# Chunked cross-attention on one core: masks added on VectorE with the score copy, row maximum subtracted on GpSimd

## The chip, the core and the metric

One core of a Trainium2 chip runs the whole program. The metric is the device time of one execution in microseconds. Five engines work side by side, each with its own in-order queue: TensorE (PE, matmuls and its weight loads PEld), VectorE (DVE), ScalarE (ACT), GpSimd (POOL) and SyncE (SP, which issues all DMAs here). Engines wait for each other through semaphores that count completed instructions.

## The reference

The inputs are x and ctx (32 batches, 256 channels, 2048 tokens), a mask (32, 1, 2048), and the weights and biases of the projections. Tokens attend within chunks of 64, with 8 heads of 32 channels.

```
q, k, v = ctx^T W_in^T + b_in                      # 256 channels each
s   = q k^T / sqrt(32) + (0 where mask > 0 else -1e9)   # per chunk of 64 tokens and head
out = softmax(s) v ;  out = (out W_out^T + b_out) * mask + x
out = (out - mean) * rsqrt(var + 1e-5)             # mean and var over the 2048 tokens of a channel
```

## The kernel before, in words

A batch is cut into 4 blocks of 512 tokens, and each block into 2 units of 256 tokens (4 chunks). There are 8 units `u` in a batch, 256 in the run, and 128 blocks. Every engine runs the same outer loop (`batches`, `steps`): one step for each unit `u`, with work for neighbouring units and blocks. With `j = u // 2`, a step with even `u` is called an even step here, and one with odd `u` an odd step. The projections are full-size matmuls in three terms (high times high, low times high, high times low parts); scores, transposes and probabilities times values are small float32 matmuls.

TensorE's queue in step u: the scores of unit u+1 (mask rows L327, then 64 matmuls L334 into the four banks of `score_bank`); in an even step the keys of block j+1 (`project_k`, L262, two halves f=0 and 1), in an odd one the output projection of block j-1 (`project_out`, L310, two halves); probabilities times values of unit u-1 (L368); the transposes of unit u (`turn`, L349, into the other half of each score bank); in an even step the values of block j+1 (`project_v`, L293, two halves), in an odd one the queries of block j+2 (`project_q`, L262). Half f of `project_v` waits for `k_f_done` of half f, because it writes the bank that `keys` empties. `project_out` f waits for the copies of the values out of that bank (`v_done[f]`). `project_q` f waits for `y_done` of half f and for `ctx_lo`. The scores of a unit wait until the transposed probabilities of the unit two before have been copied (`prob_t_done`).

ScalarE's queue, which the diff doesn't touch:

```python
if u >= BLOCKS: normalise(B, u - BLOCKS, 0)      # L462
if h == 0: keys(B, j + 1, 0)                     # L443
exponentials(B, u + 1)                           # L412
if h == 0: keys(B, j + 1, 1)                     # L443
high_attention(B, u - 1)                         # L429, o_hi
turned_probs(B, u)                               # L419, prob_t
split_ctx(B, j + 2, 1) if h == 0 else split_ctx(B, j + 3, 0)   # L404
if u >= BLOCKS: normalise(B, u - BLOCKS, 1)      # L462
values(B, j + 1) if h == 0 else both queries(B, j + 2, f)      # L452 or L436
```

VectorE's queue in step u: `less_maximum` of unit u+1 (reduce L572, then subtraction L576, both reading the scores from PSUM); in an even step `masked_keys` (L565) and `statistics` (two L623; after it, at u = 2, `mean_and_variance`), in an odd one `output` for both halves (L614); `low_attention` of unit u-1 (L594, waits for `o_hi`); `reciprocal_sums` of unit u+1 (L583, waits for the exponentials, then L587); in an even step the copy of half of the values (L603); at u = 3 `mean_shift` (L640, L642), which waits for GpSimd's `rstd`.

GpSimd's queue in step u: at u = 3 first `reciprocal_std` (L531); in an even step two `add_residual` (L525) and `low_ctx(j+2, 1)` (L515), in an odd one `low_ctx(j+3, 0)`; then `divide` of unit u+1 (L508). `low_ctx` waits for ScalarE's `split_ctx` of the same part.

Of the kernel before, what the change touches and what calls it, by code (L numbers as in the profile page):

```python
# [5 lines left out]
F32 = mybir.dt.float32  # L6
F32R = mybir.dt.float32r
BF16 = mybir.dt.bfloat16
# [30 lines left out]
def attention_kernel(nc, x, ctx_in, mask, w_in_t, b_in, w_out_t, b_out, out):  # L39
    stack = ExitStack()  # L40
    with stack:
# [22 lines left out]
        ones_row = sb("ones_row", [P, CHUNK], BF16)  # L64
# [8 lines left out]
        neg_rows = sb("neg_rows", [P, 2, BLOCK], BF16)  # L73
# [45 lines left out]
        rows_done = sem("rows_done")  # L119
        max_done = sem("max_done")  # L120
# [129 lines left out]
        def _(pe):  # L250
# [63 lines left out]
            def scores(B, u):  # L314
# [3 lines left out]
                if h == 0:  # L318
                    pe.wait_ge(neg_done, count(B, BLOCKS, j + 1))
                    pe.wait_ge(q_f_done, count(B, 2 * BLOCKS, 2 * (j + 1)))  # L320
                    pe.wait_ge(k_f_done, count(B, 2 * BLOCKS, 2 * (j + 1)))
                wait(pe, less_done, count(B, UNITS, u))
                wait(pe, prob_t_done, count(B, UNITS, u - 1))
                for r in range(ROWS):
                    masked = neg_rows[r * DH:r * DH + 1, j % 2, h * UNIT:(h + 1) * UNIT]
                    for f in range(HALVES):
                        pe.matmul(score_bank[f * CHUNK:(f + 1) * CHUNK, r, row_part], ones_row[r * DH:r * DH + 1, :],  # L327
                                  masked, start=True, stop=False, skip_group_check=True)
                for c in range(CPU):
                    tokens = slice(h * UNIT + c * CHUNK, h * UNIT + (c + 1) * CHUNK)  # L330
                    for r in range(ROWS):
                        head = slice(r * DH, (r + 1) * DH)
                        for f in range(HALVES):
                            last = pe.matmul(score_bank[f * CHUNK:(f + 1) * CHUNK, r, c * CHUNK:(c + 1) * CHUNK],  # L334
                                             q_f[head, j % 2, f, tokens], k_f[head, j % 2, f, tokens], start=False,
                                             stop=(c == CPU - 1), skip_group_check=True)
                last.then_inc(rows_done, 1)

            def turn(B, u):
# [4 lines left out]
                if unit_there(B, u + 1):  # L344
                    pe.wait_ge(less_done, count(B, UNITS, u + 2))
# [28 lines left out]
            pe.wait_ge(pool_const, 4)  # L374
# [119 lines left out]
        def _(pool):  # L494
# [5 lines left out]
            pool.memset(ones_row[:, :], 1.0).then_inc(pool_const, 1)  # L500
            pool.wait_ge(pool_const, 4)

            def divide(B, u):
# [4 lines left out]
                pool.tensor_tensor(part, part, slots(recip[:, u % 2, :]), ALU.mult).then_inc(norm_done, 1)  # L508

# [23 lines left out]
            def steps(B):  # L533
                for u in range(UNITS):
                    j, h = u // UPB, u % UPB
                    if u == 3:
                        reciprocal_std(B)
                    if h == 0:
                        add_residual(B, j - 2, 0)
                        add_residual(B, j - 2, 1)  # L540
# [3 lines left out]
                    divide(B, u + 1)  # L544
# [4 lines left out]
        def _(dve):  # L549
# [10 lines left out]
            def masked_keys(B, n):  # L560
# [3 lines left out]
                wait(dve, rows_done, count(B, UNITS, UPB * (n - 1)))  # L564
# [3 lines left out]
            def less_maximum(B, u):  # L568
                if not unit_there(B, u):
                    return  # L570
                dve.wait_ge(rows_done, count(B, UNITS, u + 1))
                dve.tensor_reduce(row_max[:, :].rearrange("p (r c) -> p r c", c=CPU), rows, AX_X,  # L572
                                  ALU.max).then_inc(max_done, 1)
                wait(dve, turned, count(B, UNITS, u - 1))
                dve.wait_ge(max_done, count(B, UNITS, u + 1))
                dve.tensor_tensor(prob[:, u % 2, :, :, :], rows, slots(row_max[:, :]),  # L576
                                  ALU.subtract).then_inc(less_done, 1)
# [109 lines left out]
```

## Time and profile before

| | |
|---|---|
| median of 3 runs | 2226.42 us (2226.14 to 2228.15) |
| profiled execution, its own time | 2225.78 us |
| its span, first to last instruction | 2224.0 us |
| PE busy | 2189.0 us (98%) |
| DVE busy | 1755.9 us (79%) |
| ACT busy | 1380.2 us (62%) |
| POOL busy | 1149.8 us (52%) |
| mean granted TensorE clock | 0.997 |

The table's busy times overlap, since the engines run side by side. In the timelines below each row gives the start in microseconds from the start of the span, the duration, the engine, the line of the kernel, the operation, the tensors (out<-in), the shapes, and a count where equal instructions that touch are merged. A bracket at the end is idle time of the engine just before the row, with what ended it.

### The profile page before, as it was taken

The page shows a single profiled execution, that of the slowest core. Times are in us where ns is not written, and L with a number is a line of the kernel's source. Part 1 is how long each engine was busy: PE and PEld are TensorE (multiplying, and loading weights), DVE is VectorE, ACT ScalarE, POOL GpSimd, SP SyncE. Part 2 cuts the span into 40 slices and gives each one's busy share as a digit, 9 for nine tenths or more (in the row PEclk, how much of TensorE's full clock was granted, in tenths as well). Part 3 has the DMA queues.
Part 4 walks back from the last instruction along what each step waited for, and adds up shares of the span by engine and source line. Part 5 has one row for each costly group of instructions (what it writes and reads, how often), then busy time and mean ns, then how long its engine had stood idle before and what let it go on. Part 6 is the DMA issues. An engine that isn't in the chain of part 4 may idle for free.

```text
span 2224.0 us, 97930 instructions
## 1 busy us (share of the span) xinstructions
PE 2189.0 (98%) x44552; PEld 1835.7 (83%) x44552; DVE 1755.9 (79%) x2213; ACT 1380.2 (62%) x1921; POOL 1149.8 (52%) x808
## 2 busy tenths in 40 slices
PE   7999999999999999999999999999999999999996
PEld 6888888888888888888888888888888888888885
DVE  4778877887878788778887788787788877887875
ACT  4566566666666666666666666666666566666664
POOL 3455555555555555455545554555455555555553
PEclk9999999999999999999999999999999999999998
DMA  3223333323333233333333332333333333323322
GB/s 133 79 93 113 114 111 111 120 98 104 109 121 121 93 108 120 112 115 115 102 103 111 120 121 88 111 114 118 116 102 108 110 111 112 121 97 108 107 92 96
DMA packets 126172, 242.23 MB, mean 109 GB/s; under 512 B 10561, under 2 KB 10817, under 8 KB 125761
## 3 DMA queue, kind: packets, MB, share of 16 engines
q1 hardware_dynamic: 125760, 235.97, 32.6%
q8 instruction: 352, 5.77, 1.1%
q14 instruction: 60, 0.48, 0.1%
HBM read 168.82 MB, written 67.11 MB: 106 GB/s over the span
## 4 chain that ended last, share of the span: by engine, by line
PE 97%; DVE 1%; ACT 1%; issue 0%; POOL 0%; DMA 0%; SPq 0%; POOLq 0%; ACTq 0%; DVEq 0%
PE proj_bank L262 33%; PE proj_bank L310 17%; PE proj_bank L293 16%; PE score_bank L349 12%; PE o_bank L368 9%; PE score_bank L334 8%; PE score_bank L327 3%; DMA ctx_raw<-ctx 0%; ACT y L462 0%; POOL prob L508 0%; POOL y L525 0%; DVE prob L576 0%; DVE row_max L572 0%; POOL ctx_lo L515 0%; DVE o_lo L594 0%
## 5 line engine op out<-in xcount | busy, mean ns | idle before, releaser
L515 POOL TENSOR_TENSOR ctx_lo<-ctx_raw,ctx_hi 128x512 fp32r<-128x512 f32 x256 | 330.3, 1291 | 1032.4 <-ACT ctx_hi L404 1032.4
L572 DVE TENSOR_REDUCE row_max<-score_bank 128x16 f32<-128x1024 f32 x256 | 313.3, 1224 | 305.0 <-PE score_bank L334 305.0
L412 ACT ACTIVATE prob<-prob 128x1024 f32<-128x1024 f32 x256 | 271.0, 1058 | 380.0 <-DVE prob L576 380.0
L508 POOL TENSOR_TENSOR prob<-prob,recip 128x1024 f32<-128x1024 f32 x256 | 487.0, 1902 | 23.1 <-DVE recip L587 20.9
L262 PE MATMUL proj_bank<-ctx_hi,w_hi 128*128 128x512 f32 x1024 | 342.4, 416 | 5.1 <-POOL ctx_lo L515 4.3
L576 DVE TENSOR_TENSOR prob<-score_bank,row_max 128x1024 f32<-128x1024 f32 x256 | 313.6, 1225 | 28.4 <-DVE row_max L572 2.4
L525 POOL TENSOR_TENSOR y<-y,x_raw 128x512 f32<-128x512 f32 x256 | 324.4, 1287 | 7.5 <-DVE y L614 7.4
L262 PE MATMUL proj_bank<-ctx_hi,w_lo 128*128 128x512 f32 x1024 | 317.8, 391 | 0.0
L262 PE MATMUL proj_bank<-ctx_lo,w_hi 128*128 128x512 f32 x1024 | 316.7, 391 | 0.0
L583 DVE TENSOR_REDUCE sums<-prob 128x16 f32<-128x1024 f32 x256 | 308.8, 1206 | 1.9 <-ACT prob L412 1.9
L419 ACT ACTIVATE prob_t<-score_bank 128x1024 f32<-128x1024 f32 x256 | 263.0, 1027 | 59.6 <-PE score_bank L349 53.6
L443 ACT ACTIVATE k_f<-proj_bank,b_cols 128x512 f32<-128x512 f32 x256 | 174.1, 680 | 193.0 <-PE proj_bank L262 193.0
L349 PE MATMUL score_bank<-ident,prob 128*128 128x128 f32 x2048 | 279.5, 279 | 3.9 <-DVE prob L576 3.9
L368 PEld LDWEIGHTS o_bank<-prob_t,v_f 64*32 64x32 f32 x16384 | 178.4, 105 | 91.0 <-issue 90.8
L349 PEld LDWEIGHTS score_bank<-ident,prob 128*128 128x128 f32 x2048 | 219.7, 141 | 27.6 <-issue 4.2
L334 PE MATMUL score_bank<-k_f,q_f 32*64 32x64 f32 x16384 | 230.7, 228 | 0.0
L594 DVE TENSOR_TENSOR o_lo<-o_bank,o_hi 128x512 fp32r<-128x512 f32 x256 | 174.5, 682 | 67.8 <-ACT o_hi L429 67.7
L262 PEld LDWEIGHTS proj_bank<-ctx_hi,w_lo 128*128 128x128 f32 x1024 | 192.9, 188 | 42.1
L262 PEld LDWEIGHTS proj_bank<-ctx_lo,w_hi 128*128 128x128 f32 x1024 | 192.7, 188 | 42.0
L334 PEld LDWEIGHTS score_bank<-k_f,q_f 32*64 32x64 f32 x16384 | 222.0, 130 | 0.3
L368 PE MATMUL o_bank<-prob_t,v_f 64*32 64x64 f32 x16384 | 219.8, 224 | 1.2 <-ACT prob_t L419 1.2
L293 PE MATMUL proj_bank<-w_hi,ctx_hi 128*128 128x256 f32 x1024 | 216.5, 293 | 0.0
(45 smaller groups left out, 3457.9 us busy)
## 6 DMA issues: line engine op xcount, KB each, us to landing
ctx_raw<-ctx SPq DMA_DIRECT2D x128, 512.0 KB, 5.1
x_raw<-x SPq DMA_DIRECT2D x128, 512.0 KB, 4.2
out<-y SPq DMA_DIRECT2D x256, 256.0 KB, 2.7
mask_all<-mask SPq DMA_DIRECT2D x128, 256.0 KB, 3.5
y<-w_in_t SPq DMA_DIRECT2D x1, 768.0 KB, 4.3
y<-w_out_t SPq DMA_DIRECT2D x1, 256.0 KB, 4.5
b_cols<-b_in SPq DMA_DIRECT2D x1, 3.0 KB, 4.2
bo_cols<-b_out SPq DMA_DIRECT2D x1, 1.0 KB, 4.9
```

The lines of the kernel that those rows point to most:

```text
L262: last = pe.matmul(proj_bank[:, f, :], w[:, h, col + f * P:col + (f + 1) * P], c[:, n % 2, h, :], start=(a == 0 and h == 0), stop=(a == 2 ...
L293: last = pe.matmul(proj_bank[:, f, t * C:(t + 1) * C], c[:, n % 2, h, tok:tok + P], w[:, h, 2 * C:3 * C], start=(a == 0 and h == 0), stop= ...
L310: last = pe.matmul(proj_bank[:, f, :], w[:, h, f * P:(f + 1) * P], o[:, m % 2, :, h, :], start=(a == 0 and h == 0), stop=(a == 2 and h == 1))
L334: last = pe.matmul(score_bank[f * CHUNK:(f + 1) * CHUNK, r, c * CHUNK:(c + 1) * CHUNK], q_f[head, j % 2, f, tokens], k_f[head, j % 2, f, t ...
L349: last = pe.transpose(score_bank[:, r, at:at + P], prob[:, u % 2, r, 2 * t:2 * t + 2, :].rearrange("p c k -> p (c k)"), ident[:, :])
L368: last = pe.matmul(o_bank[r * DH:(r + 1) * DH, c, at:at + CHUNK], v_f[keys, j % 2, h, t, values], prob_t[keys, u % 2, r, t, f, :], start=T ...
L508: pool.tensor_tensor(part, part, slots(recip[:, u % 2, :]), ALU.mult).then_inc(norm_done, 1)
L515: pool.tensor_tensor(ctx_lo[:, n % 2, :, tokens], ctx_raw[:, n % BLOCKS, :, tokens], ctx_hi[:, n % 2, :, tokens].bitcast(F32), ALU.subtrac ...
L525: pool.tensor_tensor(part, part, x_raw[:, m % 2, f, :], ALU.add).then_inc(added, 1)
L572: dve.tensor_reduce(row_max[:, :].rearrange("p (r c) -> p r c", c=CPU), rows, AX_X, ALU.max).then_inc(max_done, 1)
L576: dve.tensor_tensor(prob[:, u % 2, :, :, :], rows, slots(row_max[:, :]), ALU.subtract).then_inc(less_done, 1)
L583: dve.tensor_reduce(sums[:, :], prob[:, u % 2, :, :, :].rearrange("p r c k -> p (r c) k"), AX_X, ALU.add).then_inc(sums_done, 1)
```

## The change

The mask is no longer accumulated into the scores by TensorE: the 8 mask matmuls for each unit (L327) and `ones_row` are gone, and `neg_rows` is held in float32. VectorE adds the mask rows while it copies the scores from PSUM to `prob` in SBUF (`masked_scores`, first instruction), and then takes the row maximum from `prob` (second instruction). GpSimd subtracts the maximum in place in `prob` (the new GpSimd `less_maximum`), and ScalarE's exponentials wait for that. GpSimd's order in a step becomes: `divide` of unit u, in an even step `add_residual` f=0, `less_maximum` of unit u+1, in an even step `add_residual` f=1, `low_ctx`, and at u = 3 `reciprocal_std` at the very end. VectorE's `statistics` move from even to odd steps, ahead of `output`, and `mean_and_variance` from u = 2 to u = 3. TensorE's scores and transposes wait for `masked_done` in place of `less_done`; `less_done` now counts GpSimd's subtractions. The reduce, the exponential, the sums and the division by them keep their shapes.

```diff
-                    pe.wait_ge(neg_done, count(B, BLOCKS, j + 1))
-                wait(pe, less_done, count(B, UNITS, u))
+                wait(pe, masked_done, count(B, UNITS, u))
-                for r in range(ROWS):
-                    masked = neg_rows[r * DH:r * DH + 1, j % 2, h * UNIT:(h + 1) * UNIT]
-                    for f in range(HALVES):
-                        pe.matmul(score_bank[f * CHUNK:(f + 1) * CHUNK, r, row_part], ones_row[r * DH:r * DH + 1, :],
-                                  masked, start=True, stop=False, skip_group_check=True)
-                                             q_f[head, j % 2, f, tokens], k_f[head, j % 2, f, tokens], start=False,
-                                             stop=(c == CPU - 1), skip_group_check=True)
+                                             q_f[head, j % 2, f, tokens], k_f[head, j % 2, f, tokens], start=True,
+                                             stop=True, skip_group_check=True)
...
-                    pe.wait_ge(less_done, count(B, UNITS, u + 2))
+                    pe.wait_ge(masked_done, count(B, UNITS, u + 2))
...
+            def less_maximum(B, u):                      # GpSimd
+                pool.wait_ge(max_done, count(B, UNITS, u + 1))
+                part = prob[:, u % 2, :, :, :]
+                pool.tensor_tensor(part, part, slots(row_max[:, :]), ALU.subtract).then_inc(less_done, 1)
...
             def steps(B):                                # GpSimd
                 for u in range(UNITS):
-                    if u == 3:
-                        reciprocal_std(B)
+                    divide(B, u)
                     if h == 0:
                         add_residual(B, j - 2, 0)
+                    less_maximum(B, u + 1)
+                    if h == 0:
                         add_residual(B, j - 2, 1)
                         low_ctx(B, j + 2, 1)
                     else:
                         low_ctx(B, j + 3, 0)
-                    divide(B, u + 1)
+                    if u == 3:
+                        reciprocal_std(B)
...
+            def masked_scores(B, u):                     # VectorE
+                if h == 0:
+                    dve.wait_ge(neg_done, count(B, BLOCKS, j + 1))
+                dve.wait_ge(rows_done, count(B, UNITS, u + 1))
                 wait(dve, turned, count(B, UNITS, u - 1))
+                dve.tensor_tensor(prob[...], score_bank[:, :, row_part], neg_rows[...broadcast over ROWS],
+                                  ALU.add).then_inc(masked_done, 1)
+                dve.wait_ge(masked_done, count(B, UNITS, u + 1))
+                dve.tensor_reduce(row_max[:, :], prob[...], AX_X, ALU.max).then_inc(max_done, 1)
...
             def steps(B):                                # VectorE
                 for u in range(UNITS):
-                    less_maximum(B, u + 1)
+                    masked_scores(B, u + 1)
                     if h == 0:
                         masked_keys(B, j + 1)
+                    else:
                         statistics(B, j - 2)
-                        if u == 2:
+                        if u == 3:
                             mean_and_variance(B)
-                    else:
                         output(B, j - 1, 0)
                         output(B, j - 1, 1)
                     low_attention(B, u - 1)
```

## Rows read from the trace of the kernel before

**Rows 1.** The page: shares of the chain that ended last, by engine.

```profile
PE 97%; DVE 1%; ACT 1%; issue 0%; POOL 0%; DMA 0%; SPq 0%; POOLq 0%; ACTq 0%; DVEq 0%
```

**Rows 2.** Timeline of PE alone, one block in mid-run (even step, then odd).

```profile
1032.41 0.32 PE L327 MATMUL score_bank<-neg_rows,ones_row 1*64 1x256 bf16 x8
1032.54 0.90 PE L334 MATMUL score_bank<-k_f,q_f 32*64 32x64 f32 x64
...
1037.95 0.48 PE L293 MATMUL proj_bank<-w_hi,ctx_hi 128*128 128x256 f32 x2
...
1041.00 0.32 PE L327 MATMUL score_bank<-neg_rows,ones_row 1*64 1x256 bf16 x8
...
1041.96 0.73 PE L310 MATMUL proj_bank<-o_hi,wo_hi 128*128 128x512 f32 x2
...
1046.54 0.71 PE L262 MATMUL proj_bank<-ctx_hi,w_hi 128*128 128x512 f32 x2
...
1049.45 0.32 PE L327 MATMUL score_bank<-neg_rows,ones_row 1*64 1x256 bf16 x8
```

**Rows 3.** Timeline of VectorE in the same block.

```profile
1035.95 1.38 DVE L565 TENSOR_SCALAR neg_rows<-mask_all 128x512 bf16<-128x512 f32 x1
...
1040.34 0.25 DVE L587 RECIPROCAL recip<-sums 128x16 f32<-128x16 f32 x1
1040.51 0.63 DVE L603 COPY v_f<-proj_bank 128x512 f32<-128x512 f32 x1
1042.07 1.23 DVE L572 TENSOR_REDUCE row_max<-score_bank 128x16 f32<-128x1024 f32 x1 [0.93 <-PE score_bank L334]
1043.40 1.23 DVE L576 TENSOR_TENSOR prob<-score_bank,row_max 128x1024 f32<-128x1024 f32 x1
1044.54 1.40 DVE L614 SCALAR_TENSOR_TENSOR y<-proj_bank,b_final,mask_all 128x512 f32<-128x512 f32 x2
1046.43 0.69 DVE L594 TENSOR_TENSOR o_lo<-o_bank,o_hi 128x512 fp32r<-128x512 f32 x1 [0.49 <-ACT o_hi L429]
1047.03 1.21 DVE L583 TENSOR_REDUCE sums<-prob 128x16 f32<-128x1024 f32 x1
1048.35 0.25 DVE L587 RECIPROCAL recip<-sums 128x16 f32<-128x16 f32 x1
```

**Rows 4.** Timeline of ScalarE in the same block.

```profile
1036.07 1.06 ACT L412 ACTIVATE prob<-prob 128x1024 f32<-128x1024 f32 x1 [0.31 <-DVE prob L576]
1037.03 0.67 ACT L443 ACTIVATE k_f<-proj_bank,b_cols 128x512 f32<-128x512 f32 x1
1037.60 0.59 ACT L429 ACTIVATE o_hi<-o_bank 128x512 fp32r<-128x512 f32 x1
1038.23 1.03 ACT L419 ACTIVATE prob_t<-score_bank 128x1024 f32<-128x1024 f32 x1
1039.15 0.62 ACT L404 ACTIVATE ctx_hi<-ctx_raw 128x512 fp32r<-128x512 f32 x1
...
1044.65 1.06 ACT L412 ACTIVATE prob<-prob 128x1024 f32<-128x1024 f32 x1 [2.25 <-DVE prob L576]
```

**Rows 5.** Timeline of GpSimd in the same block.

```profile
1032.64 1.90 POOL L508 TENSOR_TENSOR prob<-prob,recip 128x1024 f32<-128x1024 f32 x1
1034.51 2.54 POOL L525 TENSOR_TENSOR y<-y,x_raw 128x512 f32<-128x512 f32 x2
1039.85 1.29 POOL L515 TENSOR_TENSOR ctx_lo<-ctx_raw,ctx_hi 128x512 fp32r<-128x512 f32 x1 [2.81 <-ACT ctx_hi L404]
1041.11 1.90 POOL L508 TENSOR_TENSOR prob<-prob,recip 128x1024 f32<-128x1024 f32 x1
```

**Rows 6.** Instructions of one line: durations min/median/max (ns), first and last start.

```profile
L642 DVE TENSOR_SCALAR shift<-shift x32: 168/1106/1836, 128.4 to 2215.2; 128x2 f32<-128x2 f32 x32
...
L565 DVE TENSOR_SCALAR neg_rows<-mask_all x128: 416/1379/1443, 13.3 to 2178.4; 128x512 bf16<-128x512 f32 x128
```

**Rows 7.** Groups by line: busy us, mean ns, idle before.

```profile
L531 POOL TENSOR_TENSOR rstd<-var_eps,minus_half 128x2 f32<-128x2 f32 x32 | 22.4, 700 | 1.4 <-DVE var_eps L634 1.4
```

**Rows 8.** Busy us by stretch (PE, PEld, DVE, ACT, POOL), granted clock, DMA share.

```profile
2190.00:2224.00 34.00, 14.10 (x304) 10.75 (x304) 14.57 (x24) 14.19 (x20) 12.05 (x9) 0.78 0.34 117
```

More of the change, by code:

```diff
@@ L7 @@
 F32R = mybir.dt.float32r
-BF16 = mybir.dt.bfloat16
 ALU = mybir.AluOpType
@@ L119, in attention_kernel @@
         rows_done = sem("rows_done")
+        masked_done = sem("masked_done")
         max_done = sem("max_done")
@@ L373, in _ @@
             pe.wait_ge(dve_const, 5)
-            pe.wait_ge(pool_const, 4)
+            pe.wait_ge(pool_const, 3)
             def steps(B):
@@ L508, in divide @@
                 pool.tensor_tensor(part, part, slots(recip[:, u % 2, :]), ALU.mult).then_inc(norm_done, 1)
+            def less_maximum(B, u):
+                if not unit_there(B, u):
+                    return
+                pool.wait_ge(max_done, count(B, UNITS, u + 1))
+                part = prob[:, u % 2, :, :, :]
+                pool.tensor_tensor(part, part, slots(row_max[:, :]), ALU.subtract).then_inc(less_done, 1)
             def low_ctx(B, n, part):
@@ L563, in masked_keys @@
                 dve.wait_ge(mask_loaded[n % BLOCKS], count(B, 16, 16 * (n // BLOCKS + 1)))
-                wait(dve, rows_done, count(B, UNITS, UPB * (n - 1)))
                 dve.tensor_scalar(neg_rows[:, n % 2, :], mask_all[:, n % BLOCKS, :], 0.0, -BIG, ALU.is_le,
                                   ALU.mult).then_inc(neg_done, 1)
-            def less_maximum(B, u):
+            def masked_scores(B, u):
                 if not unit_there(B, u):
                     return
+                j, h = u // UPB, u % UPB
+                if h == 0:
+                    dve.wait_ge(neg_done, count(B, BLOCKS, j + 1))
                 dve.wait_ge(rows_done, count(B, UNITS, u + 1))
-                dve.tensor_reduce(row_max[:, :].rearrange("p (r c) -> p r c", c=CPU), rows, AX_X,
-                                  ALU.max).then_inc(max_done, 1)
                 wait(dve, turned, count(B, UNITS, u - 1))
-                dve.wait_ge(max_done, count(B, UNITS, u + 1))
-                dve.tensor_tensor(prob[:, u % 2, :, :, :], rows, slots(row_max[:, :]),
-                                  ALU.subtract).then_inc(less_done, 1)
+                dve.tensor_tensor(prob[:, u % 2, :, :, :].rearrange("p r c k -> p r (c k)"),
+                                  score_bank[:, :, row_part],
+                                  neg_rows[:, j % 2, h * UNIT:(h + 1) * UNIT].unsqueeze(1).broadcast_to(
+                                      [P, ROWS, UNIT]), ALU.add).then_inc(masked_done, 1)
+                dve.wait_ge(masked_done, count(B, UNITS, u + 1))
+                dve.tensor_reduce(row_max[:, :], prob[:, u % 2, :, :, :].rearrange("p r c k -> p (r c) k"),
+                                  AX_X, ALU.max).then_inc(max_done, 1)
             def reciprocal_sums(B, u):
```

6 lines of the change are left out of this document (2 added, 4 removed).

## The prediction

> **What bounds the kernel now.** I read the page first: the chain that ended last is TensorE's for 97% [rows 1]. Then the timelines of one block, engine by engine. A block lasts from one even step's mask matmuls to the next's, 1032.41 to 1049.45, 17.04 us: 8.59 for the even step and 8.45 for the odd [rows 2]. TensorE has no bracket of idle time in it; VectorE and ScalarE do, ahead of L572 and L412 [rows 3, 4], and GpSimd ahead of L515 [rows 5]. So TensorE sets the pace, and the question is how far each other queue may slip before it takes over.
>
> **TensorE's part.** From the first mask matmul to the first score matmul is 0.13 us [rows 2]. Taking L327 away gives at most that, since the eight run beside each other: 0.26 a block, 33 us over 256 units. The period would fall to 16.78. The start and stop flags cost nothing: the same 64 matmuls are left.
>
> **VectorE's part.** The add reads PSUM and one SBUF operand and writes 1024 elements, like L576, 1.23 us; the reduce moves to SBUF, like L583, 1.21 us for the same 1024 elements [rows 3]. A dependent successor starts 0.10 after an end (L572 to L576), an independent one 0.08 to 0.09 ahead of it. So the pair takes as long as the old one. L565 keeps its length; I come to its wait below.
>
> **GpSimd's part.** The subtraction has the form of L508 (1024 elements in place, second operand with a stride of zero): 1.90 us, 256 times, 487 us. GpSimd goes from 1150 to about 1640 us, which would still fit. I take 1.90; lower is 1.23, VectorE's time for the same elements, and above I allow 2.54, two L525 of 512 elements, in which neither operand is broadcast [rows 3, 5]. Of the elementwise work the Trainium skill (GPSIMD Engine Reference, 3.1) says that GpSimd needs 1.96 times VectorE's time with two inputs. By that the subtraction would be 1.96 x 1.23 = 2.40, an estimate, and the sum below some 128 us more; the row of the same form says 1.90, and the row decides.
>
> The subtraction doesn't lie beside other work of its unit. It lies between the maximum and the exponential: before, the exponential started 0.02 after L576 ended (1044.63 to 1044.65); now it starts 0.08 (crossing to GpSimd, L404's end 1039.77 to L515's start 1039.85) + 1.90 + 0.03 = 2.01 us after the maximum [rows 3 to 5]. Three in-order queues stand behind it.
>
> I follow one block, with time 0 at the start of the even step's subtraction.
>
> *ScalarE, even step.* Exponential at 1.93. Behind it in the queue, at the distances of [rows 4]: second keys half +0.96 at 2.89, done 3.57; o_hi +0.57 at 3.46, done 4.05; prob_t at 3.96; split_ctx +0.92 at 4.88, done 5.50. The second half of `project_v` waits for those keys: it can't start before 3.62.
>
> *VectorE.* L594 waits for o_hi: 4.09. Then L583 +0.60 at 4.69, L587 +1.31 at 6.00, the copy L603 +0.17 at 6.17 (done 6.80), and only then the next step's add at 6.72, reduce +1.33 at 8.05, maximum at 9.26 [rows 3]. The odd step's subtraction: 9.34.
>
> *GpSimd between.* Residual f=1 1.9 to 3.15; `low_ctx` after split_ctx at 5.58, `divide` at 5.58 + 1.26 = 6.84, done 8.74 [rows 5]. It is free by 9.34.
>
> *Odd step.* Exponential at 11.27; o_hi 12.23 (+0.96), prob_t 12.73, split_ctx 13.65, done 14.27 [rows 4]. GpSimd: `low_ctx` 14.35, `divide` +1.26 at 15.61, residual f=0 +1.87 at 17.48, and the next even step's subtraction +1.25 at 18.73 [rows 5]. VectorE alone (o_hi done 12.82, L594, L583, L587 at 14.77) would have a maximum ready earlier, so GpSimd's order decides: `divide` is queued behind a `low_ctx` that waits for ScalarE, and the subtraction behind `divide` and a residual.
>
> The loop closes at **18.73 us**, with TensorE outside it. TensorE fits in: the second half of `project_v` at 3.62 needs half of the 3.05 of L293 (1037.95 to 1041.00), plus 0.08, so the odd step starts at about 5.23; its `project_out` would follow at 6.06 (0.83 from L334 on) but waits for the copy L603, 6.85; from there 7.49 to the next step (1041.96 to 1049.45) gives 14.34 [rows 2]. `project_q`, 4.58 behind `project_out` (1041.96 to 1046.54), comes at 11.43; it needs the first output. With statistics now ahead of it that ends at 11.1, 0.3 in time. TensorE's two idle stretches are 1.1 us ahead of the second half of `project_v`, and 0.8 ahead of `project_out`: 16.78 + 1.1 + 0.8 is the same 18.7.
>
> **L565.** It takes 0.42 at its shortest and 1.38 in the median [rows 6], and in this block it ended (1037.33) 0.28 after the second residual (1037.05) [rows 3, 5]: it waits for a GpSimd instruction to end. Now it comes up while residual f=0 runs, and the subtraction stands next. If VectorE gets in first, as L565 did, the subtraction is up to 0.28 later; if not, 0. Nothing of it was excluded by a row; I take 0.2: 18.93. The Trainium skill (SBUF — State Buffer, on the shared port pair) has it as an exclusive lock for a whole instruction; by it the full 0.28 counts, an estimate of 10 us more than mine, and the rows agree on the blocking.
>
> **Once a batch, mean_shift.** `reciprocal_std` now stands behind `low_ctx` at u = 3: 15.61 to 16.31 (700 ns, [rows 7]). VectorE waits there, then L642 meets `divide` of the next unit, which started at 16.27. L642 had to wait before too: 168 ns at its shortest, 1106 in the median behind an L515, 1836 once, the length of an L508 [rows 6]. So VectorE is free at 18.2; add, reduce, and the subtraction at about 20.8, perhaps 0.1 more for L565. That block lasts 20.9. If L642 gets in at once the block has only the 0.70 of L531 in GpSimd's queue, 19.6; if it misses a second GpSimd instruction, 22.1.
>
> **The sum.** Four blocks: 3 x 18.93 + 20.9 = 77.7, 19.42 each against 17.04, +2.38. L565 runs 128 times between 13.3 and 2178.4, so some 127 blocks pass at this pace: +302. The tail is bound by the chain of each last unit; some three subtractions of 1.90 lie bare there: +6. Against the profiled execution of 2225.8 (span 2224.0, and 0.6 below the median of 2226.4): 2225.8 + 308 = **2534**. Bounds: no wait for L565 and none for L642 gives 127 x (18.95 - 17.04) = 243, 2475; 0.28 and 22.1 give 127 x (19.8 - 17.04) = 350, 2582. If links of the loop, some 20 with 0.02 read from each row, err one way, that is 0.2 to 0.3 a block, 30 us.
>
> **Rivals.**
> *The gain comes through (faster).* If the block's order leaves slack for the two microseconds, TensorE keeps the pace at 16.78 and the time is 2226 - 33 = 2193. It decides on one place: the second keys half must be out by the time `project_v` wants it, half of its 3.05 us after L293's start. Before, that half was done at 1037.70 and wanted at 1039.48 [rows 2, 4]: 1.78 of slack against the 1.99 that the subtraction and its crossing add, even with GpSimd free. It needs a subtraction below 1.7 us, and a GpSimd that is free each time. 1.23 would give the first of these. Chance 0.05.
> *Only that place costs.* If GpSimd were always free when the maximum is ready, the block would be 17.04 - 0.26 + 0.3 or so: no more than 17.2, and the time 2230 to 2250. Loops that overlap more than I read would lie between this and my case, up to 2460. Against it: `divide` has to follow `low_ctx` in the queue. Chance 0.10, 0.03 of it within 0.2% of before.
> *TensorE's clock.* The granted clock is 1.00 in mid-run, and 0.78 over the last 34 us, where TensorE was busy for 14.10 [rows 8], so part of that stretch was at 1.2 GHz and not 2.4. Now TensorE would be busy for 16.8 of 19.4, and once a batch idle for some 3 us on end. If each batch lost a stretch, each microsecond of matmuls at half speed costs one more; 3 to 5 a batch is 100 to 160 us, 2630 to 2700. Chance 0.05.
> *GpSimd slower than its row.* With 2.40 for the subtraction, twice in the loop, +1.0 a block: 2660. For it speaks only that VectorE works beside it more often. Chance 0.02. The Trainium skill's rate (same page and section) is the source of this case.
>
> **How the numbers follow.** My case has 0.78, with 2475 to 2600 as its own range. To leave out no more than 2 in 10 the range is 2465 to 2610. A measurement of this kernel can't tell less than about 0.2% from nothing. Faster has the first rival's 0.05, within 0.2% 0.03, slower 0.92.
>
> **What would show it.** TensorE: idle ahead of L293 near 1.1 us a block for `keys`, and ahead of L310 near 0.8 for the copy of the values; its share of the final chain far below 97%. GpSimd: idle ahead of `low_ctx` for split_ctx, none to speak of ahead of `divide` or the even steps' subtraction. VectorE idle ahead of `low_attention` for o_hi rather than ahead of the add for scores. L642 near 1.9 us, blocks about 18.9 apart, and 20.9 once in four. Wrong would be: an add that waits for L334, GpSimd idle ahead of the even subtraction, or a subtraction far from 1.90.

## The result and the profile after

The changed kernel takes 2554.65 us in the median (2553.09 to 2555.74) against 2226.28 before: a ratio of 1.147, with a 95% interval of 1.145 to 1.149. The forecast was 2534, with 2465 to 2610 as its range. The profiled execution has a span of 2554.0 us. In the experiments further down one execution of e8_keys_first_rstd_early took 3293.27 us, at a mean granted clock of 0.557, and its time there is the median of the other three.

I read the profile after in the order of before. First the page, the final chain by engine and by line.

```profile
POOL 36%; DVE 20%; issue 16%; PE 14%; ACT 13%; ACTq 0%; DMA 0%; DVEq 0%; SPq 0%; POOLq 0%
POOL prob L507 20%; PE proj_bank L292 9%; DVE row_max L582 8%; DVE prob L576 7%; POOL prob L500 7%; POOL y L524 5%; PE score_bank L327 4%; POOL ctx_lo L514 4%; ACT k_f L436 3%; ACT ctx_hi L397 3%; ACT o_hi L422 3%; ACT prob_t L412 3%; DVE v_f L609 3%; DVE shift L646 2%; POOL rstd L530 1%
```

TensorE's share has gone from 97% [rows 1] to 14%. The new subtraction (L507) leads, but no engine fills the chain: it goes round through four of them. Then one block of GpSimd's timeline, from one even step's subtraction (1032.86) to the next (1051.66).

```profile
1031.62 1.30 POOL L524 TENSOR_TENSOR y<-y,x_raw 128x512 f32<-128x512 f32 x1
1032.86 2.10 POOL L507 TENSOR_TENSOR prob<-prob,row_max 128x1024 f32<-128x1024 f32 x1
1034.92 1.29 POOL L524 TENSOR_TENSOR y<-y,x_raw 128x512 f32<-128x512 f32 x1
1038.62 1.27 POOL L514 TENSOR_TENSOR ctx_lo<-ctx_raw,ctx_hi 128x512 fp32r<-128x512 f32 x1 [2.41 <-ACT ctx_hi L397]
1039.85 1.91 POOL L500 TENSOR_TENSOR prob<-prob,recip 128x1024 f32<-128x1024 f32 x1
1042.32 1.91 POOL L507 TENSOR_TENSOR prob<-prob,row_max 128x1024 f32<-128x1024 f32 x1 [0.56 <-DVE row_max L582]
1047.31 1.28 POOL L514 TENSOR_TENSOR ctx_lo<-ctx_raw,ctx_hi 128x512 fp32r<-128x512 f32 x1 [3.08 <-ACT ctx_hi L397]
1048.54 1.91 POOL L500 TENSOR_TENSOR prob<-prob,recip 128x1024 f32<-128x1024 f32 x1
1050.41 1.29 POOL L524 TENSOR_TENSOR y<-y,x_raw 128x512 f32<-128x512 f32 x1
1051.66 2.08 POOL L507 TENSOR_TENSOR prob<-prob,row_max 128x1024 f32<-128x1024 f32 x1
```

The block lasts 18.80 us, where it lasted 17.04 [rows 2]. The brackets tell what each instruction waited for. The odd step's subtraction waits for the maximum. The even step's has no bracket: it follows `divide` (L500) and a residual (L524) without a gap, and `divide` follows `low_ctx` (L514), which waits for ScalarE. The even subtraction takes 2.10 and the odd one 1.91.

ScalarE in the same block: exponential, second half of the keys, o_hi; then the exponential and split_ctx of the odd step.

```profile
1034.99 1.06 ACT L405 ACTIVATE prob<-prob 128x1024 f32<-128x1024 f32 x1 [2.82 <-POOL prob L507]
1035.96 0.67 ACT L436 ACTIVATE k_f<-proj_bank,b_cols 128x512 f32<-128x512 f32 x1
1036.53 0.59 ACT L422 ACTIVATE o_hi<-o_bank 128x512 fp32r<-128x512 f32 x1
...
1044.26 1.06 ACT L405 ACTIVATE prob<-prob 128x1024 f32<-128x1024 f32 x1 [3.83 <-POOL prob L507]
...
1046.60 0.63 ACT L397 ACTIVATE ctx_hi<-ctx_raw 128x512 fp32r<-128x512 f32 x1
```

VectorE at the start of the block (L565), and then from o_hi to the next maximum, where it has no idle time to speak of:

```profile
1032.12 1.07 DVE L565 TENSOR_SCALAR neg_rows<-mask_all 128x512 f32<-128x512 f32 x1
...
1037.15 0.69 DVE L600 TENSOR_TENSOR o_lo<-o_bank,o_hi 128x512 fp32r<-128x512 f32 x1 [3.95 <-ACT o_hi L422]
1037.75 1.21 DVE L589 TENSOR_REDUCE sums<-prob 128x16 f32<-128x1024 f32 x1
1039.07 0.25 DVE L593 RECIPROCAL recip<-sums 128x16 f32<-128x16 f32 x1
1039.24 0.63 DVE L609 COPY v_f<-proj_bank 128x512 f32<-128x512 f32 x1
1039.78 1.21 DVE L576 TENSOR_TENSOR prob<-score_bank,neg_rows 128x1024 f32<-128x1024 f32 x1
1041.02 1.22 DVE L582 TENSOR_REDUCE row_max<-prob 128x16 f32<-128x1024 f32 x1
```

And TensorE's two waits of the block, for the keys and for the copy of the values:

```profile
1036.68 0.50 PE L292 MATMUL proj_bank<-w_hi,ctx_hi 128*128 128x256 f32 x2 [0.61 <-ACT k_f L436]
...
1040.01 0.71 PE L309 MATMUL proj_bank<-o_hi,wo_hi 128*128 128x512 f32 x2 [0.80 <-DVE v_f L609]
```

Once a batch the block is longer. The start of the step after u = 3, on GpSimd:

```profile
1086.14 0.70 POOL L530 TENSOR_TENSOR rstd<-var_eps,minus_half 128x2 f32<-128x2 f32 x1
1086.80 1.91 POOL L500 TENSOR_TENSOR prob<-prob,recip 128x1024 f32<-128x1024 f32 x1
1088.66 1.29 POOL L524 TENSOR_TENSOR y<-y,x_raw 128x512 f32<-128x512 f32 x1
1092.43 2.01 POOL L507 TENSOR_TENSOR prob<-prob,row_max 128x1024 f32<-128x1024 f32 x1 [2.48 <-DVE row_max L582]
```

and on VectorE:

```profile
1086.87 1.85 DVE L646 TENSOR_TENSOR shift<-mean_var,rstd 128x2 f32<-128x2 f32 x1 [1.28 <-POOL rstd L530]
1088.76 1.22 DVE L648 TENSOR_SCALAR shift<-shift 128x2 f32<-128x2 f32 x1
1089.89 1.21 DVE L576 TENSOR_TENSOR prob<-score_bank,neg_rows 128x1024 f32<-128x1024 f32 x1
...
1092.27 0.42 DVE L565 TENSOR_SCALAR neg_rows<-mask_all 128x512 f32<-128x512 f32 x1
```

Each of the two shift instructions works on two elements. L646 ends (1088.72) as `divide` ends (1088.71), and L648 ends (1089.98) as the residual does (1089.95). Each has waited for nearly the whole of a GpSimd instruction. This block ran from 1070.44 to 1092.43, 21.99 us. The four blocks from 1032.86 on take 18.80, 18.78, 21.99 and 18.73. Over the run the starts of L565 are 19.60 us apart (52.1 to 2502.1 in 125 blocks), against 17.05 before: 125 x 2.55 = 319 of the 328 us; the other 9 lie at the start and the end of the run.

### The profile page after: what moved, and what is told of

Its sections match the earlier page's. It is cut to its first block, busy times and chain, and to the rows that moved or that the text cites. A ratio compares the mean times of both kernels' runs of the same rounds, so it can differ in the third digit from the quotient of the medians.

```text
span 2554.0 us, 93964 instructions
## 1 busy us (share of the span) xinstructions
PE 2239.6 (88%) x42504; PEld 1825.8 (71%) x42504; DVE 1760.5 (69%) x2213; ACT 1320.5 (52%) x1921; POOL 1648.6 (65%) x1063
## 4 chain that ended last, share of the span: by engine, by line
POOL 36%; DVE 20%; issue 16%; PE 14%; ACT 13%; ACTq 0%; DMA 0%; DVEq 0%; SPq 0%; POOLq 0%
POOL prob L507 20%; PE proj_bank L292 9%; DVE row_max L582 8%; DVE prob L576 7%; POOL prob L500 7%; POOL y L524 5%; PE score_bank L327 4%; POOL ctx_lo L514 4%; ACT k_f L436 3%; ACT ctx_hi L397 3%; ACT o_hi L422 3%; ACT prob_t L412 3%; DVE v_f L609 3%; DVE shift L646 2%; POOL rstd L530 1%
## 5 line engine op out<-in xcount | busy, mean ns | idle before, releaser
L514 POOL TENSOR_TENSOR ctx_lo<-ctx_raw,ctx_hi 128x512 fp32r<-128x512 f32 x256 | 326.2, 1275 | 711.6 <-ACT ctx_hi L397 711.6
L507 POOL TENSOR_TENSOR prob<-prob,row_max 128x1024 f32<-128x1024 f32 x256 | 508.3, 1986 | 160.1 <-DVE row_max L582 160.1
L500 POOL TENSOR_TENSOR prob<-prob,recip 128x1024 f32<-128x1024 f32 x256 | 488.0, 1906 | 12.7 <-DVE recip L593 12.7
L292 PE MATMUL proj_bank<-w_hi,ctx_hi 128*128 128x256 f32 x1024 | 233.1, 310 | 136.1 <-ACT k_f L436 135.9
L576 DVE TENSOR_TENSOR prob<-score_bank,neg_rows 128x1024 f32<-128x1024 f32 x256 | 310.9, 1215 | 55.0 <-PE score_bank L327 47.0
L524 POOL TENSOR_TENSOR y<-y,x_raw 128x512 f32<-128x512 f32 x256 | 328.7, 1284 | 8.4 <-DVE y L620 8.4
L261 PE MATMUL proj_bank<-ctx_lo,w_hi 128*128 128x512 f32 x1024 | 322.6, 396 | 0.0
L582 DVE TENSOR_REDUCE row_max<-prob 128x16 f32<-128x1024 f32 x256 | 312.4, 1220 | 8.8
L292 PEld LDWEIGHTS proj_bank<-w_hi,ctx_hi 128*128 128x128 f32 x1024 | 159.6, 193 | 162.3 <-ACT k_f L436 162.2
L455 ACT ACTIVATE y<-y,shift,rstd 128x512 f32<-128x512 f32 x256 | 208.3, 817 | 120.5 <-DVE shift L648 120.5
L309 PE MATMUL proj_bank<-o_hi,wo_hi 128*128 128x512 f32 x512 | 172.0, 417 | 98.8 <-DVE v_f L609 94.0
L327 PEld LDWEIGHTS score_bank<-k_f,q_f 32*64 32x64 f32 x16384 | 199.4, 131 | 68.7 <-issue 52.7
L327 PE MATMUL score_bank<-k_f,q_f 32*64 32x64 f32 x16384 | 234.6, 231 | 3.9 <-ACT prob_t L412 3.9
```

The lines of the kernel that those rows point to most:

```text
L261: last = pe.matmul(proj_bank[:, f, :], w[:, h, col + f * P:col + (f + 1) * P], c[:, n % 2, h, :], start=(a == 0 and h == 0), stop=(a == 2 ...
L292: last = pe.matmul(proj_bank[:, f, t * C:(t + 1) * C], c[:, n % 2, h, tok:tok + P], w[:, h, 2 * C:3 * C], start=(a == 0 and h == 0), stop= ...
L507: pool.tensor_tensor(part, part, slots(row_max[:, :]), ALU.subtract).then_inc(less_done, 1)
L514: pool.tensor_tensor(ctx_lo[:, n % 2, :, tokens], ctx_raw[:, n % BLOCKS, :, tokens], ctx_hi[:, n % 2, :, tokens].bitcast(F32), ALU.subtrac ...
L524: pool.tensor_tensor(part, part, x_raw[:, m % 2, f, :], ALU.add).then_inc(added, 1)
L576: dve.tensor_tensor(prob[:, u % 2, :, :, :].rearrange("p r c k -> p r (c k)"), score_bank[:, :, row_part], neg_rows[:, j % 2, h * UNIT:(h ...
```

## The experiments

The first four kernels ran on one chip (before: 2228.66 us), the next four on another (2227.30), the last three on a third (2229.57). Each ratio is against before on the same chip. The changed kernel was timed with the before of 2226.28 us, so a difference in us between kernels of two chips is uncertain by some 3 us.

**e1_no_mask_matmuls.** From the kernel before; the mask isn't added.

```diff
-                for r in range(ROWS):
-                    masked = neg_rows[...]
-                    for f in range(HALVES):
-                        pe.matmul(score_bank[...], ones_row[...], masked, start=True, stop=False, ...)
...
-                                             ..., start=False, stop=(c == CPU - 1), ...)
+                                             ..., start=True, stop=True, ...)
```

> The kernel before, with the mask matmuls left out and nothing put in their place, so the mask isn't added to the scores (all else as before). This is TensorE's part of the change alone. My theory: 0.13 us a unit, the block falls from 17.04 to 16.78 and the time from 2226 to about 2193, since every other queue has slack. Rival: TensorE loses the saving to a wait for another queue even here, and the time stays at 2215 to 2227; then the after kernel's loss wouldn't be due to the subtraction's place alone.

Measured: 2206.45 us, 0.990 (0.9885 to 0.9915), TensorE still at 97% of the final chain. TensorE's part is a gain, but of 22 us and not 33: the ordinary block is 16.83, and the mean over the run 16.87. From the first score matmul to the next projection it was 0.83 us before. Now it is 0.84 in most units, and 1.03 or 1.04 in 31 of the 256, once a batch; what costs 0.2 there wasn't looked for. The rival falls: 22 of 33 us come through, and the time is below its 2215.

**e2_rstd_early.** From the changed kernel: the waits of mean_shift.

```diff
                     less_maximum(B, u + 1)
+                    if u == 3:
+                        reciprocal_std(B)
...
-                    if u == 3:
-                        reciprocal_std(B)
...
+                    if u == 3:
+                        mean_shift(B)
                     low_attention(B, u - 1)
                     reciprocal_sums(B, u + 1)
                     if h == 0:
                         values(B, j + 1)
-                    if u == 3:
-                        mean_shift(B)
```

> The changed kernel, with GpSimd's reciprocal_std directly behind the subtraction at u = 3 (ahead of low_ctx) and VectorE's mean_shift ahead of low_attention, both in idle time of their engines. My theory: of the 21.99 us of the block in which mean_shift stands, 3.2 are its waits for rstd and for two GpSimd instructions; they go, each block lasts 18.8, and the time falls by 32 x 3.2 = 102 us to about 2452. Rival: GpSimd's load is what counts, then moving 0.7 us within its queue is worth at most 32 x 0.7 = 22 us, 2532.

Measured: 2456.13 us, 1.102 (1.100 to 1.104), against 2452 expected. VectorE's two instructions now find GpSimd idle:

```profile
1118.60 0.14 DVE L646 TENSOR_TENSOR shift<-mean_var,rstd 128x2 f32<-128x2 f32 x1
1118.78 0.17 DVE L648 TENSOR_SCALAR shift<-shift 128x2 f32<-128x2 f32 x1
```

and the block with mean_shift lasts 18.81. So 98 of the 328 us come from two instructions of two elements and their wait for `rstd`, once a batch, at the wrong moment.

**e3_keys_first.** From the changed kernel, one ScalarE instruction moved.

```diff
-                    exponentials(B, u + 1)
                     if h == 0:
                         keys(B, j + 1, 1)
+                    exponentials(B, u + 1)
```

> The changed kernel, with ScalarE's second keys half ahead of the exponentials instead of behind them. My theory: the keys half takes 0.57 us of queue between the exponential and o_hi, in the loop once a block, and the wait of TensorE ahead of the second half of project_v goes: 127 x 0.57 = 72 us less, about 2482. The loop over GpSimd's order stays. Rival 1: TensorE's stalls for the keys are themselves the loss (0.61 to 2.43 us a block, 136 us in all), then they come back whole: 2420. Rival 2: only GpSimd's queue counts, then nothing changes: 2555.

Measured: 2509.64 us, 1.126 (1.125 to 1.128): 45 us less, not 72. Most ordinary blocks took what was forecast, 18.15 to 18.24, but the block behind the one with mean_shift took up to 20.2. The stretches below are a block with mean_shift, a longer one behind it, and an ordinary one, twice (busy us of PE, PEld, DVE, ACT, POOL; then the granted clock).

```profile
1127.30:1149.30 22.00, 19.62 (x408) 15.93 (x407) 16.69 (x22) 10.39 (x16) 14.30 (x10) 1.00 0.20 62
1149.30:1168.50 19.20, 16.34 (x261) 13.41 (x260) 12.50 (x17) 11.39 (x16) 12.65 (x8) 0.91 0.31 97
1168.50:1186.00 17.50, 16.81 (x333) 13.87 (x332) 12.25 (x17) 10.95 (x16) 11.86 (x9) 1.00 0.36 103
...
1204.20:1226.20 22.00, 19.61 (x408) 15.90 (x407) 16.68 (x22) 10.38 (x15) 14.31 (x10) 1.00 0.19 62
1226.20:1246.30 20.10, 17.43 (x261) 14.07 (x260) 12.47 (x17) 11.40 (x16) 12.63 (x8) 0.83 0.30 94
1246.30:1263.80 17.50, 16.78 (x333) 13.86 (x332) 12.26 (x17) 10.93 (x16) 11.85 (x9) 1.00 0.30 98
```

In the longer blocks the granted clock is 0.91 and 0.83, so part of each was at 1.2 GHz; it comes after TensorE had idled for 1.93 us ahead of the scores and up to 0.94 ahead of the output projection, some 2 us apart. The whole trace agrees. From 125 us on, 30 blocks follow one with mean_shift: 26 of them have time at the lower clock and take 18.91 to 20.20 us, the other four have none and take 18.14. The 26 are 37 us longer in all than at 18.14. Neither rival fits: 45 us are less than the 136 of TensorE's stalls for the keys, and more than nothing.

**e4_residuals_after.** From the changed kernel, one GpSimd instruction moved.

```diff
                     divide(B, u)
-                    if h == 0:
-                        add_residual(B, j - 2, 0)
                     less_maximum(B, u + 1)
                     if h == 0:
+                        add_residual(B, j - 2, 0)
                         add_residual(B, j - 2, 1)
```

> The changed kernel, with both add_residual behind the subtraction, so that the subtraction follows divide directly. GpSimd does the same work. My theory: in the even step the subtraction waits for the maximum (ready 0.5 to 0.6 us before GpSimd takes it now) instead of for the residual, and the block is about 18.2; where mean_shift stands, L648 no longer waits behind a residual, 1.2 us less. Together 3 x 0.55 + 1.2 to 1.3 a batch, 32 times: some 95 us less, 2460. Rival: GpSimd's load counts and not its order, then the time stays at 2555.

Measured: 2475.29 us, 1.111 (1.109 to 1.113): 79 us less with the same work, 15 short of the forecast. The ordinary block is 18.13, a little under the forecast. The one with mean_shift is 20.88, 1.1 less than 21.99: the second shift instruction takes 0.17 us in it and no longer 1.22, while the first still takes 1.85. But 17 of the other blocks are longer, 18.4 to 20.4, some 16 us in all. Nine of them, each behind a block with mean_shift, have time at the lower clock; the other eight have none, and what made them longer stays open. The rival, load without order, falls.

**e5_subtract_on_vector.** From the changed kernel: the subtraction on VectorE.

```diff
                                   AX_X, ALU.max).then_inc(max_done, 1)
+                dve.wait_ge(max_done, count(B, UNITS, u + 1))
+                part = prob[:, u % 2, :, :, :]
+                dve.tensor_tensor(part, part, slots(row_max[:, :]), ALU.subtract).then_inc(less_done, 1)
...
-                    less_maximum(B, u + 1)          # GpSimd's steps
```

> The changed kernel, with the subtraction done on VectorE right behind the reduce (in place in SBUF) and not on GpSimd; all orders as in the changed kernel. My theory: the loop through GpSimd opens, since the exponential starts 1.3 us after the maximum instead of 2.0 and the subtraction no longer stands behind divide and a residual. VectorE's odd step is now longer ahead of output (add, reduce, subtract, statistics), so project_q waits some 1.1 us: a block of about 18.0, or some 2360, and up to 1.3 us a block more if the in-place subtraction with its two SBUF inputs has to wait for a running GpSimd instruction (up to 2500). Rival: the loss lies only in GpSimd's load (487 us more), then this falls to 2206, the time with no mask matmuls.

Measured: 2463.63 us, 1.106 (1.104 to 1.108). It takes 494 us of busy time off GpSimd (1154.8 against 1648.6) and gives back only 91. The mean of the moved instruction and the waits of TensorE's queue:

```profile
L578 DVE TENSOR_TENSOR prob<-prob,row_max 128x1024 f32<-128x1024 f32 x256 | 370.5, 1447 | 8.8
```

```profile
PE proj_bank L261 <- DVE y L615: 100.7, 123, 1.3
PE proj_bank L309 <- DVE v_f L604: 98.0, 123, 1.2
```

`project_q` waits 0.8 us a block for the output behind statistics, as expected, and the subtraction with two SBUF inputs takes 1.72 in most even steps, where it starts while a residual runs, and 1.22 in odd ones. What my 2360 had left out is the second of these waits, for the copy of the values, 0.8 us a block, which this kernel keeps: some 100 us, about what lies between 2360 and 2464. The rival, 2206, is far off.

**e6_more_gpsimd.** From the changed kernel, more GpSimd work in its idle time.

```diff
...
+                    wait(pool, extra_done, count(B, UNITS, u) + UNITS)
+                    pool.tensor_tensor(scratch[:, 1, :], scratch[:, 0, :], scratch[:, 0, :], ALU.add).then_inc(
+                        extra_done, 1)
                     if h == 0:
                         low_ctx(B, j + 2, 1)
```

> The changed kernel, with one more GpSimd instruction in each step (a 512-element add of zeros into a scratch tile that nobody reads, about 1.3 us, 256 of them, 330 us in all), placed just ahead of low_ctx, where GpSimd is idle for 2.4 and 3.1 us. My theory: GpSimd's load isn't the bound but its place in the chain, so the time stays within 0.3% of 2555. Rival: GpSimd's load or its sharing of SBUF with VectorE costs in proportion: at 1650 us busy against 330 more, 2600 to 2880.

Measured: 2557.09 us, 1.148 (1.146 to 1.150), the same as the changed kernel. The added instruction:

```profile
1044.04 1.04 POOL L545 TENSOR_TENSOR scratch<-scratch 128x512 f32<-128x512 f32 x1
```

It took 1.04 us and not 1.3, and ran 272 times and not 256: GpSimd is busy for 272 us more, 1920.8 against 1648.6. Its load can grow by that much, put in the right place, for nothing.

**e7_new_orders.** From the changed kernel: the same instructions, the queues re-ordered.

```diff
+                    if h == 0:                       # ScalarE
+                        split_ctx(B, j + 2, 1)
+                    else:
+                        split_ctx(B, j + 3, 0)
                     if u >= BLOCKS:
                         normalise(B, u - BLOCKS, 0)
                     if h == 0:
                         keys(B, j + 1, 0)
-                    exponentials(B, u + 1)
-                    if h == 0:
                         keys(B, j + 1, 1)
                     high_attention(B, u - 1)
+                    exponentials(B, u + 1)
                     turned_probs(B, u)
-                    if h == 0:
-                        split_ctx(B, j + 2, 1)
-                    else:
-                        split_ctx(B, j + 3, 0)
...
                     divide(B, u)                     # GpSimd
                     if h == 0:
-                        add_residual(B, j - 2, 0)
-                    less_maximum(B, u + 1)
-                    if h == 0:
-                        add_residual(B, j - 2, 1)
                         low_ctx(B, j + 2, 1)
                     else:
                         low_ctx(B, j + 3, 0)
+                    less_maximum(B, u + 1)
                     if u == 3:
                         reciprocal_std(B)
+                    if h == 0:
+                        add_residual(B, j - 2, 0)
+                        add_residual(B, j - 2, 1)
...
+                        output(B, j - 1, 0)          # VectorE, odd steps
+                        output(B, j - 1, 1)
                         statistics(B, j - 2)
                         if u == 3:
                             mean_and_variance(B)
-                        output(B, j - 1, 0)
-                        output(B, j - 1, 1)
                     low_attention(B, u - 1)
+                    if u == 3:
+                        mean_shift(B)
                     reciprocal_sums(B, u + 1)
                     if h == 0:
                         values(B, j + 1)
-                    if u == 3:
-                        mean_shift(B)
```

> The changed kernel with the same instructions in other orders. ScalarE: split_ctx first in the step, both keys halves, then high_attention, then the exponentials, then the copy of the transposes. GpSimd: divide, low_ctx, subtraction, (u = 3: reciprocal_std), both residuals. VectorE: output ahead of statistics, mean_shift ahead of reciprocal_sums. My theory: nothing of the next step is then queued behind the exponential that needn't be, TensorE is the bound again, and the time is that of the kernel with no mask matmuls, 2200 to 2215, below before's 2228. Rival: the 2.0 us more between maximum and exponential can't be hidden whatever the order; then it stays above 2240.

Measured: 2219.84 us, 0.9966 (0.9954 to 0.9978), faster than before by a third of a per cent. GpSimd is as busy as in the changed kernel (1653 us). The page, the chain by engine:

```profile
PE 96%; POOL 1%; DVE 1%; issue 1%; ACT 1%; DMA 0%; SPq 0%; POOLq 0%; ACTq 0%; DVEq 0%
```

The bound is TensorE again, and the whole loss was order. It is 5 us above what I had given as its upper end, and 13 above e1.

**e8_keys_first_rstd_early.** e2 and e3 together.

> e2_rstd_early and e3_keys_first together. In e3 the ordinary block was 18.21 as forecast, but after each block with mean_shift (22.0 us, TensorE idle for more than 2 us on end) one or two blocks took 18.9 to 20.2. My theory: that is TensorE at the lower of its two clocks after the long idle stretch; with the stretch gone all blocks take about 18.2, the granted clock is 0.99, and the time is 2456 - 127 x 0.57 = 2384. Rival: the longer blocks come from the order of the keys itself; then they stay, and the time is 2384 + 32 x 1.3 = 2425.

Measured: 2382.47 us, 1.070 (1.068 to 1.071), against 2384; the granted clock is 0.994, and the long blocks of e3 are gone. The two edits are worth 98 and 45 alone, and 172 together. The 29 between fit the clock: the blocks at the lower clock cost e3 37 us, by the sum above, and the changed kernel some 7 (nine blocks of some 19.5 where the other 21 behind mean_shift's take 18.72). In e8 none is left in mid-run.

**e9_new_orders_pad, e10_before_shifted, e11_changed_pad.** Taking `ones_row` away had moved the SBUF tensors allocated behind it 128 bytes lower, up to `neg_rows`, which is now twice as large. The padding, or `ones_row` allocated last, moves every tensor behind that place by 128 bytes.

```diff
+        pad = sb("pad", [P, CHUNK // 2], F32)          # e9 (from e7) and e11 (from the changed kernel)
         minus_half = sb("minus_half", [P, HALVES], F32)
...
-        ones_row = sb("ones_row", [P, CHUNK], BF16)    # e10 (from the kernel before)
...
         shift = sb("shift", [P, HALVES], F32)
+        ones_row = sb("ones_row", [P, CHUNK], BF16)
```

> e7_new_orders with an unused tile of 128 bytes a partition where ones_row stood, so that the tensors behind it (ctx_hi, ctx_lo, q_f, k_f, v_f) begin at the addresses of the kernel before; nothing else differs. In e7 TensorE is the bound again, but its 512-column matmuls start 231 ns apart and not 227 as in the kernel before, which makes up most of its 13 us above the kernel without mask matmuls. Theory A: the addresses do it; then the distance is 227 again and the time falls by about 12 us to 2208. Theory B: the other engines' greater SBUF traffic does it (GpSimd 487 us more); then nothing changes, 2220.

> The kernel before, with ones_row allocated last instead of ahead of minus_half, so that the same tensors lie 128 bytes lower, as in the changed kernel; the instructions are the same. Theory A (addresses): the 512-column matmuls start 231 ns apart instead of 227, 0.05 to 0.1 us a block of 36 of them and more, and the time rises by 0.3 to 0.7%, 2234 to 2243. Theory B (traffic): nothing changes.

> The changed kernel with the same 128-byte tile. TensorE isn't in its loop over most of a block, so whichever theory holds for the 4 ns, the time stays within 0.5% of 2555. If the addresses cost TensorE on the path too, it falls by the same 12 us.

Measured: e9 2212.31 us, 0.992 (0.991 to 0.994), the fastest version here with the mask added; e10 2238.00, 1.004 (1.003 to 1.006); e11 2553.76, 1.145 (1.144 to 1.147). The twelve matmuls of `project_q` and the switch to the scores, from TensorE's timeline, in e7,

```profile
1045.36 0.71 PE L261 MATMUL proj_bank<-ctx_hi,w_hi 128*128 128x512 f32 x2
...
1048.32 0.91 PE L327 MATMUL score_bank<-k_f,q_f 32*64 32x64 f32 x64
```

in e9,

```profile
1041.40 0.71 PE L262 MATMUL proj_bank<-ctx_hi,w_hi 128*128 128x512 f32 x2
...
1044.31 0.91 PE L328 MATMUL score_bank<-k_f,q_f 32*64 32x64 f32 x64
```

and in e10:

```profile
1033.96 0.71 PE L262 MATMUL proj_bank<-ctx_hi,w_hi 128*128 128x512 f32 x2
...
1036.92 0.32 PE L327 MATMUL score_bank<-neg_rows,ones_row 1*64 1x256 bf16 x8
```

2.96 us in e7 and e10, and 2.91 in e9 as before [rows 2]: the addresses decide, in both directions. The ordinary block goes the same way, from 16.90 in e7 to 16.83 in e9, and from 17.04 before to 17.12 in e10. Theory B falls for these matmuls. e9 gives back 7.5 us (9 by the ratios) rather than the 12 expected. It stays 6 us above e1, though the ordinary block is 16.83 in both: the rest lies in the first blocks and in one block of each batch, about 17.05 against 16.97. e11 shows that in the changed kernel, where TensorE isn't the bound, none of this matters.

## Why the prediction was right

*TensorE's part*, 33 us at most: 22 in e1. TensorE being outside the loop, this didn't reach the time.

*VectorE's part*, nothing: right. The add takes 1.22 and the reduce 1.22; a dependent successor starts 0.03 after the add's end, not 0.10.

*GpSimd's 1.90 and the 2.0 us crossing*: right, 1.91 where nothing is in the way. The 1.96 of the Trainium skill (GPSIMD Engine Reference, 3.1), which gave 2.40, doesn't hold for this form: the measured ratio to VectorE's 1.22 is 1.57.

*The three queues behind the exponential.* With 1032.86 as zero the exponential stood at 2.13 (predicted 1.93, and 2.13 with the 0.2 for L565), o_hi at 3.67 (3.46), the copy of the values at 6.38 (6.17), the odd subtraction at 9.46 (9.34), `low_ctx` at 14.45 (14.35), `divide` at 15.68 (15.61), the next even subtraction at 18.80 (18.73, or 18.93 with L565). Single links were undone: e3 took the keys out of the loop, 18.80 to 18.21 for an ordinary block (0.57 forecast); e4 took the residual out, 18.80 to 18.13 (0.55 forecast).

*TensorE's stalls*, 1.1 and 0.8: 0.61 by its bracket and 0.80. The first is smaller because TensorE's own work from `project_out` round to the second half of `project_v` took some 0.4 us more than I had, which the stall absorbs.

*L565*: the even subtraction lasts 2.10 against 1.91, so the 0.2 that I chose stands, and lies in the subtraction's duration. VectorE got in first: L565 came up while the residual ran and ended at 1033.19, 0.27 after the residual's end (1032.92), while the subtraction had started by its record at 1032.86. The row couldn't tell this beforehand, so the 0.2 was a choice that came out well and not a result. In the block where L565 found GpSimd idle (1092.27) it took 0.42, and the subtraction behind it 2.01.

*mean_shift* was the term that was mis-sized. I gave 20.9 for its block and 22.1 as the bound "if it misses a second GpSimd instruction"; it was 21.99. I had let L640 (now L646) through at once and only L642 (now L648) wait for `divide`. In the run L646, which has two SBUF inputs, waited for `divide`, and the residual then got in ahead of L648. In the old trace the same instruction (there L640) mostly took 0.10 us, even with a GpSimd instruction running:

```profile
1082.52 1.30 POOL L515 TENSOR_TENSOR ctx_lo<-ctx_raw,ctx_hi 128x512 fp32r<-128x512 f32 x1 [4.58 <-ACT ctx_hi L404]
1082.60 0.10 DVE L640 TENSOR_TENSOR shift<-mean_var,rstd 128x2 f32<-128x2 f32 x1
```

There it started 0.08 after an instruction that GpSimd began out of idle time; in the changed kernel it started 0.07 after `divide`, which followed `rstd` without a gap, and took 1.85. The lag is nearly the same, so the idle time ahead of the GpSimd instruction is the likely difference; once in the old trace (946.32) L640 started 0.23 after such an L515, and took 1.07. No run varies this alone, so it isn't shown.

The miss is 1.1 us a batch, 33 us over the 30 batches in mid-run. The other blocks were shorter than my 18.93 (18.79, and 18.72 behind mean_shift's), 15 us the other way, and nine of those behind mean_shift's took some 19.5, partly at the lower clock, 7 us. Together that is some 26; the first and last blocks give about 5 back, which leaves the 20 between 2534 and 2555. So the period came out well within its bounds, but that the total is only 20 us off owes something to errors that cancel.

*The rivals.* Faster: the order of the queues shut it out, and e7 and e9 show that it was there to be had, with other orders. "Only that place costs" fell: `divide` follows `low_ctx` without a gap. GpSimd slower than its row: 1.91. The clock: 0.988 over the run and some 7 us in mid-run, far from the 100 to 160 of the rival, but the mechanism is real, as e3 shows (27 us of its 72 went there, and e8 got them back).

## What to carry to other kernels

When a latency is put into a chain, don't ask whether the engine that does it has the time; ask what stands behind the waiting instruction in each in-order queue, and follow it round until it comes back to itself. Here the loop through the queues gave the period to within 1% from rows of the old trace. Then move what doesn't depend on the waiting instruction ahead of it: this alone turned 15% slower into 0.3% faster than before (e7), and with the padding into 0.8% (e9). A two-element instruction of VectorE cost as much as GpSimd's longest instruction (1.85 us for L646), so put it where that engine idles (0.14 in e2).

## What the runs showed of the hardware

VectorE's L646 (two SBUF inputs, two elements) took 0.14 us with GpSimd idle and 1.85 with `divide` running. The Trainium skill (SBUF — State Buffer, Who interferes with whom) says that a VectorE instruction with two SBUF inputs contends with a GpSimd instruction that reads SBUF; these runs agree, and e5 adds a case where it starts late in a GpSimd instruction and loses 0.5 us (1.72 against 1.22). The kernel before has the exception shown above: L640, 0.08 us behind the start of an L515 that followed idle time, took 0.10. L648 has one SBUF input and waits too: 0.17 us in e2 and e4, 1.22 here.

Between two back-to-back GpSimd instructions VectorE got in with L565 (0.2 us on GpSimd's next), but not with L648, which came 0.04 us after L646, when the residual had started by its record: there the residual went first.

A shift of 128 bytes in SBUF changed the time of twelve of TensorE's 512-column matmuls (2.91 to 2.96 us) and that of the run by 0.3 to 0.4%, in both directions (e7 to e9, before to e10). Which tensors' addresses matter, and why, wasn't tried.

TensorE fell to the lower clock level in e3 after idle stretches of 1.93 and up to 0.94 us close together, in 26 of 30 batches in mid-run. In the changed kernel idle time of 2.43 us ahead of `project_v`, where it waits for the keys, once a batch, left it at 1.00 in 21 of 30. That row of the changed kernel:

```profile
1096.17 0.50 PE L292 MATMUL proj_bank<-w_hi,ctx_hi 128*128 128x256 f32 x2 [2.43 <-ACT k_f L436]
```

The same stretches come before a fall in some batches and before none in others (in e3, 1.93 and 0.94 at 692.5 and 694.4 us, with none); what tells them apart stays open.
